# Gated cross-attention and mixture of experts on one core: two layer-norm statistics moved next to each other, and the waits that follow them

## The reference, cut to what matters

```python
q  = layernorm(x) @ Wq ; k, v = split(context @ Wkv)        # one null key and value are put in front
out = softmax(q k^T / 8) v @ Wout                            # 16 heads
x1 = x + tanh(g_xattn) * (layernorm(out) * ln_scale + ln_bias)
h  = layernorm(x1)                                           # called x2 in the kernel
w  = top8(sigmoid(h @ Wr + br)), divided by its sum
y  = x1 + tanh(g_ffn) * (shared_expert(h) + sum over experts of w * expert(h))
```

## Time and profile before

| what | value |
|---|---|
| median of the runs | 2310.6 us (2310.09 to 2318.49, 3 runs) |
| the profiled execution | 2310.3 us, its span 2308.6 us |
| attention phase in the span | about 256 to 1300 us |
| TensorE busy, share of the span | 2080.1 us, 90% |
| VectorE busy | 1837.3 us, 80% |
| ScalarE busy | 1532.5 us, 66% |
| GpSimd busy | 1299.8 us, 56% |
| mean granted TensorE clock | 0.966 of full speed |

### The profile page before, as it was taken

One profiled execution on the slowest core, in us unless ns is written; L12 is line 12 of the kernel. 1 busy time (PEld: TensorE's weight loads), 2 busy tenths in 40 slices (PEclk: granted clock), 3 DMA queues, 4 the chain that ended last, 5 costly groups with the idle time before them and its releaser, 6 DMA issues. The chain is left out here.

```text
span 2308.6 us, 44550 instructions
## 1 busy us (share of the span) xinstructions
PE 2080.1 (90%) x14386; PEld 1908.5 (83%) x14386; DVE 1837.3 (80%) x4287; ACT 1532.5 (66%) x4478; POOL 1299.8 (56%) x1444
## 2 busy tenths in 40 slices
PE   8999679999999999999998599999999999999992
PEld 7888578888889899888888478988888888888881
DVE  5444357888888888888888566877999999999994
ACT  5433346676767777766766235888888887888881
POOL 1000213777777777777777540001777777777776
PEclk9999889999999999999999799999999999999996
DMA  9987489987878878787887699989999999999995
GB/s 318 322 284 263 137 281 311 323 267 256 264 263 267 265 246 264 261 266 257 267 264 243 204 389 357 298 296 303 398 405 405 402 397 393 390 398 394 395 394 170
DMA packets 385092, 708.51 MB, mean 307 GB/s; under 512 B 136380, under 2 KB 248989, under 8 KB 382397
## 3 DMA queue, kind: packets, MB, share of 16 engines
q1 hardware_dynamic: 335708, 562.99, 70.1%
q0 software_dynamic: 49152, 142.67, 16.9%
HBM read 348.18 MB, written 357.30 MB: 306 GB/s over the span
## 5 line engine op out<-in xcount | busy, mean ns | idle before, releaser
L1472 POOL DMA_INDIRECT parts<-results_dram,kept_index x512 | 531.6, 1038 | 411.2 <-DMA results_dram<-y 246.0
L776 POOL DMA_INDIRECT pages_dram<-rows,kept_index x472 | 473.2, 1003 | 138.1 <-issue 120.0
L845 ACT ACTIVATE exps<-sim,minus_max 128x78 f32<-128x78 f32 x1024 | 319.1, 355 | 37.9 <-DVE minus_max L923 35.1
L1503 ACT ACTIVATE y<-yps,row_weight 128x256 f32<-128x256 f32 x636 | 246.9, 470 | 1.2 <-PE yps L134 1.2
L845 ACT ACTIVATION_READ_ACCUMULATOR exps<-sim,minus_max 128x1 f32 x1024 | 240.3, 235 | 0.0
L1494 ACT ACTIVATE w_h<-w_raw 128x768 fp32r<-128x768 f32 x159 | 137.3, 863 | 85.4 <-DMA w_raw<-in_experts 85.3
L1681 PE MATMUL xps<-ident,xin 128*128 128x128 f32 x1272 | 168.6, 276 | 28.1 <-DVE wq_l L1543 16.0
L132 PE MATMUL yps<-w_h,hid_h 128*128 128x256 f32 x636 | 179.4, 282 | 2.1 <-ACT y L1503 2.1
L133 PE MATMUL yps<-w_h,hid_l 128*128 128x256 f32 x636 | 179.8, 283 | 0.0
L134 PE MATMUL yps<-w_l,hid_h 128*128 128x256 f32 x636 | 179.2, 282 | 0.0
L1524 ACT ACTIVATE hid_h<-hidden 128x512 fp32r<-128x512 f32 x175 | 110.2, 630 | 101.4 <-DVE hidden L1634 96.9
(11 more groups left out here) (270 smaller groups left out, 7530.8 us busy)
## 6 DMA issues: line engine op xcount, KB each, us to landing
xin<-pages_dram SPq DMA_DIRECT2D x159, 576.0 KB, 9.6
results_dram<-y SPq DMA_DIRECT2D x159, 512.0 KB, 8.8
pages_dram<-blank SPq DMA_DIRECT2D x108, 576.0 KB, 3.6
w_raw<-in_experts SPq DMA_DIRECT2D x159, 385.0 KB, 9.3
pages_dram<-blank SPq DMA_DIRECT2D x12, 1728.0 KB, 7.0
keys_h_dram<-keys_h SPq DMA_DIRECT2D x32, 624.0 KB, 5.8
keys_l_dram<-keys_l SPq DMA_DIRECT2D x32, 624.0 KB, 7.6
kT_h<-keys_h_dram SPq DMA_DIRECT2D x32, 624.0 KB, 5.6
```

What stands on the lines that cost most here:

```text
L776: pool.indirect_dma_start(dram["pages"], bass.IndirectOffsetOnAxis(ap=kept_index[:, at:at + 1].bitcast(U32), axis=0), buffer(batch)[:, k / ...
L845: last = act.activation(exps[u % 2][:, h, :], scores(u)[:, h // 4, h % 4, :], ACT.Exp, bias=minus_max[u][:, h:h + 1], accum_out=row_sum[u] ...
L1472: pool.indirect_dma_start(parts[slot(batch, t)][:, k, :], None, done, bass.IndirectOffsetOnAxis(ap=kept_index[:, at:at + 1].bitcast(U32), ...
L1503: last = act.activation(y[s][:, q, :], yps[:, q, :], ACT.Copy, scale=row_weight[s][:, q:q + 1])
```

## The change

GpSimd makes root 0 directly behind root 2, ahead of scatter 12. VectorE makes statistics 0 directly behind statistics 2, ahead of the routing pieces and of the low part of Q3. ScalarE takes the high part of PV1a ahead of `apply(2)` instead of behind it. Scores 0 and 1 wait for the low part of Q1 only, scores 2 and 3 for that of Q3 as before. No instruction is added or left out.

```diff
@@ gpsimd
                 if 1 <= b <= B:
                     make_rstd(2, b - 1)
+                if b <= B - 3:
+                    make_rstd(0, b + 2)
                 if scatters:
                     scatter(b, range(12, 13))
                 if b == B:
@@
                     scatter(b, range(LAST_PICKS))
-                if b <= B - 3:
-                    make_rstd(0, b + 2)
@@ scalar
-                    if name == "Q3" and 1 <= b <= B:
+                    if name == "PV1a" and 1 <= b <= B:
                         if b - 1 >= BUFFERS:
                             act.wait_ge(scattered[(b - 1) % BUFFERS], 16 * TT * TOPK * ((b - 1) // BUFFERS))
                         apply(2, buffer(b - 1)[:, :, 0:D], lambda t: x1[1 - par][:, t, :], b - 1)
@@ vector
                         statistics(2, lambda t: x1[1 - par][:, t, :], b - 1)
+                    if name == "T3b" and b <= B - 3:
+                        dve.wait_ge(x_loaded, 16 * (b + 2))
+                        statistics(0, lambda t: x_in[:, t, :], b + 2)
@@
-                    if name == "Q3" and b <= B - 3:
-                        dve.wait_ge(x_loaded, 16 * (b + 2))
-                        statistics(0, lambda t: x_in[:, t, :], b + 2)
@@ tensor, similarity(u, b)
-                pe.wait_ge(ring_lo, nth(EVICTED, "Q3", b - 1))
+
+                pe.wait_ge(ring_lo, nth(EVICTED, "Q3" if u // 2 else "Q1", b - 1))
```

## The result

| | kernel before | changed kernel |
|---|---|---|
| median of all runs | 2314.6 us (2310.1 to 2319.2, 4 runs) | 2349.3 us (2349.1 to 2354.1, 4 runs) |
| ratio, with its 95% interval | | 1.0158 (1.0139 to 1.0176) |
| the profiled execution, its span | 2310.3 us, 2308.6 us | 2349.1 us, 2347.3 us |
| mean granted TensorE clock | 0.966 | 0.952 |

The changed kernel is 1.6% slower. The forecast was slower, 2328 us with a range of 2304 to 2334, so the direction is right and the time lies 15 us above the range.

What follows compares the result with a forecast made beforehand. TensorE was taken to bound the 30.06 us quiet step, with about 2 us of waiting. 2310.3 + 20.9 (order of lines 803 and 937) - 3 (clock) + 0 = 2328 us, range 2304 to 2334.

Steps and rivals of the forecast that it cites:

- What the change removes: Statistics 0, root 0 and apply(0) come earlier, xn about 1.7 us, so X's 1.27 us wait goes.
- Where that gain goes: X's 1.27 us reappear before scores 2 and 3, since the exponentials do not move: 0 us gained.
- The part that costs: GpSimd 0.75 us earlier puts line 803 ahead of line 937; T3a waits longer, 1.1 us in nineteen steps: +20.9 us.
- the margin of 0.06 us: Line 803 was to start 0.06 us ahead of line 937, which would then take 1.78 instead of 0.69 us.
- rival 1: Line 803 starts just behind line 937, which runs undisturbed; no change that can be told, 2303 to 2311 us, chance 0.14.
- The clock: TensorE has slack at X and Oa, so six half-clock falls cost less: 0 to -7 us, taken as -3.
- Rival 2: X's wait really saved through an earlier maximum and exponentials: 2276 us fully, 2293 for half, chance 0.05.
- Rival 3: Statistics 0 behind a late x stops VectorE in the first steps, some 5 us: 2315 us, chance 0.03.
- Priced at nothing: Later low part of Q3 (covered by the looser scores wait), Oa, DMA, SyncE: 0; first steps -1 to +1 us.

Runs made afterwards that it cites:

- line 803 out of the way: Scatter 9 put ahead of line 803, in the changed kernel (2307.4 us) and in the kernel before (2308.7 us).
- the bad order alone: Kernel before with scatters 7 and 8 one place later each, so line 803 starts 0.05 us ahead of line 937: 2334.3 us, ratio 1.0073.
- the small delay: Changed kernel with one tiny GpSimd addition (128x2, result unused) ahead of root 1: 2314.9 us, ratio 1.0008.

## Why the prediction was right, and where it was wrong

- **What the change removes**: right. X's wait is gone, root 0 follows root 2 without a wait.
- **Where that gain goes**: right. The 34.7 us came back as 28.8 us of waits for exponentials, and the maximum stood where it had (5.26 us behind statistics 2, before 5.27). The change with line 803 out of the way gives 2307.4 against 2308.7 us.
- **The part that costs**: right in place and size, and in part by luck. Line 789 came 0.83 us earlier against statistics 2 (0.75 foretold); `z` lost its idle time; scatter 8 took 1.37 us (1.32 foretold); line 803 and line 937 met within 0.05 us. 18 steps at 1.14 us are 20.5 us, where 19 at 1.1 were foretold; T3a's waits came to 34.2 us (31 foretold), and the kernel before with the bad order alone lost 20.2 over its 24 steps. The Trainium skill (SBUF — State Buffer, section "SBUF: two separate sides") has the two engines take turns whole instructions long. The trace agrees with the turns, but the order of the starts alone did not settle them: in 16 steps line 937 started 0.01 to 0.02 us first by the records and still took 1.88 us. In those the scatter was 0.05 us longer than foretold, and with it the margin of 0.06 us was gone. By the prediction's own count they were steps of rival 1, in which line 937 runs undisturbed. That they were held as well is why every step paid, and nothing in the prediction foresaw it.
- **The clock**: this is the step that failed, "0 to -7 us in all. I take -3". It measured +16.9 us in the 24 steps. That is 19.9 of the 21 us between the forecast and the measured time; the rest is 1.3 us outside these steps less 0.4 us of the term above. The reasoning held the number of half clocks fixed at six and asked only what TensorE could lose in each. That price was nearly right: 9.0 us / 6 = 1.5 each before, 25.9 / 22 = 1.2 each after. The number was what moved, from 6 to 22. The change puts waits of 0.2 and 0.93 us, and 16 us later one of 1.4, where one of 1.27 and one of 0.2 had been, and 9 of the 22 half clocks begin in scores 3 behind the wait of 0.93, 13 behind the wait of 1.4, at T3a (3) and in the query products that follow it (10). The experiments show that it takes both: with either of the two alone the clock is near that of the kernel before.
- **Rival 1** (order held, 2303 to 2311 us) did not happen, but the small delay makes it happen: 2314.9 us, 0.36 us from the collision. Its chance of 0.14 looks low beside a margin of 0.06 us, which turned out at 0.05 in 9 steps and on the other side, by 0.01 to 0.02, in 16. **Rival 2** needed an earlier maximum, as it said: with one, and the collision out of the way, it came to 2275.4 us, where 2276 was foretold for the whole gain. **Rival 3** (a late x in the first steps, some 5 us) did not show: outside the 24 steps the two kernels differ by 1.3 us.
- **Priced at nothing**: the looser wait was rightly called cover for the late low part of Q3, worth 0.66 to 0.7 us at scores 0. What was missed is that paying those 0.7 us is better: they shorten the waits of scores 2 and 3 by about as much, delay GpSimd out of the collision, and leave no half clock. This one line of code decides between 2349 and 2296 us.

What stays open is why the clock reacts as it does. In the traces, kernels whose quiet steps had waits of at most 0.8 us in these places had no half clock in 24 steps, those with one of 0.92 or 1.27 us had 3 to 10, and 22 came with 0.93 and 1.4 us together; but 1.3 and 1.3 us, at X and T3a, gave only 6. So the length of the longest wait does not decide alone. Whether the place, the distance or the third short wait of 0.2 us makes the rest was not told apart, and each count comes from one execution.

## What to carry to other kernels

A wait taken away from the bounding engine comes back at the next thing that is late; look for that first, and move it with the same change (here the maximum, 29 us). When an engine with idle time is moved by a fraction of a microsecond, list what its large SBUF instructions will now start beside, and leave a margin to the other side on purpose: a scatter moved by one place was worth 42 us. Count how often the granted clock falls, not only what each fall costs, when waits of about a microsecond change their place.

## What the runs showed of the hardware beyond this

- Small instructions on GpSimd are held by VectorE's line 937 (128x512, two SBUF inputs) too: a 128x2 product (`shift`) takes 0.61 to 0.72 us instead of 0.20 when it starts 0.02 to 0.13 us behind one, and an indirect scatter 1.32 instead of 0.96 to 1.05 when it starts 0.20 us behind one.
- Who holds whom is not read from the two starts alone. Besides the 16 steps above there are 7 steps, in the kernel before with scatter 9 early and in the one with early maxima as well, in which line 937 started about 0.44 us into a scatter and 0.53 to 0.55 us ahead of line 803, took 2.4 us and ended 0.56 us behind the end of line 803. In the quiet step of the kernel before it started 0.53 us into a scatter and 0.54 us ahead of line 803, and took 0.69 us. Why is open.
- The same sum of waits, spread otherwise, gave another time here: 0.66 + 0.40 us at scores 0 and 3 against 0.2 + 0.92 at scores 2 and 3 is the same quiet step (30.03 and 30.01 us), but 720.8 against 737.8 us for 24 steps, with 0 against 7 half clocks and the bad order in 0 against 8 of 25 steps. The medians, 2296.4 and 2314.9 us, agree.
